# Attention: all chunks of the projected parts kept, the second part of q on GpSimd, the last head's rows moved from SBUF to SBUF, sums as rows of 64

## The chip, the cores and the metric

The kernel runs on one core of a Trainium2 chip. The metric is the device time in microseconds (us) of one execution of the whole program. Engines: TensorE (PE), VectorE (DVE), ScalarE (ACT), GpSimd (POOL) and SyncE (SP), which here only issues DMAs. SBUF and PSUM have 128 partitions.

## The reference

Eight layers act on `x`, 2048 tokens of 128 numbers: a Mamba block, a mixture of experts (MoE), causal attention, MoE, Mamba, a low-rank MLP, causal attention with ALiBi biases, and the MLP again. The change is in attention alone, which runs twice with 16 heads of 8 dimensions:

```python
q, k, v = xn @ Wq, xn @ Wk, xn @ Wv           # heads: 16 x 8 columns
dots = einsum('bhid,bhjd->bhij', q, k) * scale # second one: + alibi_bias
attn = softmax(where(causal, -inf, dots))
out  = einsum('bhij,bhjd->bhid', attn, v)
x = x + out @ Wo
```

## The kernel before

Attention cuts the 2048 tokens into four chunks of 512 (`CH`, `NC` = 4) and has three stages.

**Projection.** For each chunk `project(c)` on TensorE makes q, k and v in the PSUM tile `acc`. q and k are then written as a sum of three bf16 numbers: the first part (`first_part`) by ScalarE, what is left of it (`rest`, by `remove_first` on VectorE), the second part by ScalarE (`second`), the third part of k by VectorE (`third_of_k`) and that of q by GpSimd. The parts lie in `parts`, two chunks deep, so ScalarE waits for `stored[c - 2]` before it writes chunk c. SyncE stores each part to HBM (`store_parts`: three stores for q, one for k), waits until they have landed, and loads head 0's operands of the chunk (`load_tokens(0, ...)`) back into `q_op` and `k_op`. Then it loads heads 1 to 3.

**Heads.** For each head, a first pass of scores (`item`, tile `ps_q`) gives VectorE the row maxima (`maxes`, L1701 and L1704). TensorE starts on it after the last `project`. It visits the chunks in order, chunk c with 4(c+1) blocks. The maxima go through GpSimd, TensorE, VectorE and a DMA into `q_op`. The second pass (`scores`, tile `ps_k`) is exponentiated by ScalarE (`exps`) and multiplied by v in blocks of four (`times_v`, tile `ps_o`). ScalarE copies a finished chunk to `o_sb`; SyncE stores it to HBM (`store`). One head later `load_output` brings the head's rows back as `oT` (head dimensions on partitions) and its softmax sums as `sums`, where a partition holds one (block of 256 tokens, head) pair; one chunk uses 32 of the 128 partitions.

**Output.** The last head is loaded chunk by chunk (`load_last`). For each chunk VectorE adds the four partial sums and inverts them (`invert`), adds half of the partial rows (`add_partials`; GpSimd adds the other half into `upper`), multiplies by the spread inverses (`divide`), adds the result to `x` (`add`) and takes the norm statistics for the next layer. TensorE spreads the inverses over partitions with `sel_head` (`spread`, tile `ps_s`, L1582) and multiplies by `wo` (`output`, tile `ps_y`, L1591). `spread` and `output` of chunks 0 and 1 stand in TensorE's program between the last head's `times_v` blocks, after n = 20, 24, 28 and 32 of the 40 blocks; those of chunks 2 and 3 come after the last block.

The order on every engine is the order in which the code is written. Instructions on an engine start in that order, so a wait holds back all that is behind it.

## Time and profile before

| what | value |
|---|---|
| median of 3 runs | 2073.79 us (2072.45 to 2076.75) |
| the profiled execution | 2079.87 us, span 2077.9 us |
| TensorE busy | 1798.5 us, 87% |
| VectorE busy | 1619.0 us, 78% |
| ScalarE busy | 1117.0 us, 54% |
| GpSimd busy | 542.9 us, 26% |
| first attention | from about 520 to 1003 us of the span |
| second attention | from about 1534 to 2018 us |

The span is cut into stages with different limits, so these shares alone say little; the stages of attention have to be read one by one. In the rows below, a line has the start in us, the duration in us, the engine and line, the operation and tiles, how many were merged, and in square brackets the idle time before it and what ended that. PEld is TensorE's weight load, SPq the DMA issue on SyncE. The letters a0 and a1 in a tile's name stand for the first and the second attention.

### The profile page before, as it was taken

The page shows a single profiled execution, that of the slowest core. Times are in us where ns is not written, and L with a number is a line of the kernel's source. Part 1 is how long each engine was busy: PE and PEld are TensorE (multiplying, and loading weights), DVE is VectorE, ACT ScalarE, POOL GpSimd, SP SyncE. Part 2 cuts the span into 40 slices and gives each one's busy share as a digit, 9 for nine tenths or more (in the row PEclk, how much of TensorE's full clock was granted, in tenths as well). Part 3 has the DMA queues.
Part 4 walks back from the last instruction along what each step waited for, and adds up shares of the span by engine and source line. Part 5 has one row for each costly group of instructions (what it writes and reads, how often), then busy time and mean ns, then how long its engine had stood idle before and what let it go on. Part 6 is the DMA issues. An engine that isn't in the chain of part 4 may idle for free. (4 is left out here: it accounts for less than half of the span.)

```text
span 2077.9 us, 46457 instructions
## 1 busy us (share of the span) xinstructions
PE 1798.5 (87%) x18012; PEld 902.7 (43%) x18012; DVE 1619.0 (78%) x3425; ACT 1117.0 (54%) x2083; POOL 542.9 (26%) x560
## 2 busy tenths in 40 slices
PE   6777788999799999997899977777768999999967
PEld 2222254444255555553444422222533555555534
DVE  5899965666788999984565559999658999998665
ACT  5544423222278888885322274443342888888815
POOL 2798930000200000001000029989230000000012
PEclk9899998999689999998799979999886999999969
DMA  5333300311312222211041004443012222222200
GB/s 174 117 122 120 123 11 0 82 51 31 102 30 49 53 53 57 53 27 26 3 87 51 26 20 133 124 121 102 1 43 77 49 54 57 56 61 44 34 8 21
DMA packets 64617, 127.37 MB, mean 61 GB/s; under 512 B 15959, under 2 KB 26741, under 8 KB 62925
## 3 DMA queue, kind: packets, MB, share of 16 engines
q1 hardware_dynamic: 64108, 123.88, 23.3%
q8 instruction: 142, 2.33, 0.5%
q14 instruction: 79, 0.64, 0.1%
q10 hardware_dynamic: 288, 0.52, 0.1%
HBM read 105.74 MB, written 17.43 MB: 59 GB/s over the span
## 5 line engine op out<-in xcount | busy, mean ns | idle before, releaser
L1644 ACT ACTIVATE a_probs<-a_ps_k 128x512 f32<-128x512 f32 (+3 forms) x1280 | 598.9, 545 | 229.6 <-PE a_ps_k L1556 129.8
L1538 PE MATMUL a_ps_q<-a_k_op,a_q_op 84*32 84x512 bf16 (+7 forms) x5120 | 536.5, 366 | 29.0 <-DVE a_maxes L1701 18.8
L1704 DVE TENSOR_REDUCE a_maxes<-a_ps_q 128x1 f32<-128x512 f32 x768 | 504.1, 686 | 65.9 <-PE a_ps_q L1538 63.2
L1552 PE MATMUL a_ps_k<-a_q_op,a_k_op 87*32 87x512 bf16 (+7 forms) x5120 | 518.9, 354 | 6.2 <-DMA a_q_op<-a_max_T 2.9
L1574 PE MATMUL a_ps_o<-a_probs,a_vh 128*32 128x512 f32 (+3 forms) x2752 | 318.7, 508 | 0.8 <-ACT a_probs L1644 0.8
L1538 PEld LDWEIGHTS a_ps_q<-a_k_op,a_q_op 72*32 72x32 bf16 (+1 forms) x5120 | 187.4, 97 | 175.2 <-DVE a_maxes L1704 68.7
L1701 DVE CUSTOM_DVE_ANT_0 a_ps_q<-a_ps_q,all_c_mask_q 128x128 f32<-128x128 f32 (+3 forms) x512 | 248.0, 496 | 7.6 <-PE a_ps_q L1538 6.4
L1552 PEld LDWEIGHTS a_ps_k<-a_q_op,a_k_op 75*32 75x32 bf16 (+1 forms) x5120 | 185.7, 96 | 141.7 <-ACT a_probs L1644 84.0
L979 ACT ACTIVATE e_silu<-e_psg,all_me_b 128x512 f32<-128x512 f32 x128 | 87.8, 687 | 227.9 <-PE e_psg L911 227.9
L1784 POOL CAST a_max_parts<-a_neg_max 128x16 bf16<-128x16 f32 x32 | 6.3, 197 | 756.1 <-DVE a_neg_max L1709 756.1
L1062 DVE SCALAR_TENSOR_TENSOR e_mid<-e_psv,all_me_b,e_silu 128x512 f32<-128x512 f32 x128 | 95.7, 749 | 129.3 <-PE e_psv L913 125.4
L172 POOL TENSOR_TENSOR all_rstd<-all_var_eps,all_c_minus_half 128x4 f32<-128x4 f32 x36 | 40.1, 1114 | 503.8 <-DVE all_var_eps L161 503.8
L571 POOL TENSOR_TENSOR m0sc_read<-m0sc_state,m0sc_c_rows 128x1024 f32<-128x1024 f32 x64 | 150.3, 2360 | 11.4 <-PE m0sc_psy L490 5.8
L571 POOL TENSOR_TENSOR m1sc_read<-m1sc_state,m1sc_c_rows 128x1024 f32<-128x1024 f32 x64 | 150.2, 2358 | 9.7 <-DVE m1sc_state L536 5.5
L1556 PE MATMUL a_ps_k<-all_c_mask_k,all_c_ident_b 128*32 128x128 bf16 x2048 | 150.0, 222 | 0.9 <-issue 0.9
L536 DVE TENSOR_TENSOR_SCAN m0sc_state<-m0sc_decay,m0sc_carry,m0sc_drive 128x1024 f32<-128x1024 f32 x64 | 146.6, 2331 | 0.5 <-ACT m0sc_drive L515 0.5
L536 DVE TENSOR_TENSOR_SCAN m1sc_state<-m1sc_decay,m1sc_carry,m1sc_drive 128x1024 f32<-128x1024 f32 x64 | 146.5, 2328 | 0.4 <-ACT m1sc_drive L515 0.4
L490 PE MATMUL m0sc_psy<-m0sc_read,all_c_ident 128*128 128x512 f32 x256 | 126.1, 616 | 19.1 <-POOL m0sc_read L571 19.0
L490 PE MATMUL m1sc_psy<-m1sc_read,all_c_ident 128*128 128x512 f32 x256 | 127.5, 623 | 16.7 <-POOL m1sc_read L571 16.6
L911 PE MATMUL e_psg<-e_xT,all_me_w_T 128*128 128x512 f32 x256 | 133.9, 605 | 1.5 <-ACT e_xT L197 1.5
L913 PE MATMUL e_psv<-e_xT,all_me_w_T 128*128 128x512 f32 x256 | 132.3, 599 | 0.0
L900 PE MATMUL e_pso<-e_hid,all_me_w_T 128*128 128x512 f32 x256 | 119.2, 595 | 4.7 <-DVE e_hid L1071 4.6
(265 smaller groups left out, 2396.9 us busy)
## 6 DMA issues: line engine op xcount, KB each, us to landing
m0sc_c_rows<-m_bc_rows SPq DMA_DIRECT2D x32, 512.0 KB, 3.6
e_w_rows<-e_comb SPq DMA_DIRECT2D x64, 256.0 KB, 3.2
m1sc_c_rows<-m_bc_rows SPq DMA_DIRECT2D x32, 512.0 KB, 3.6
a_outputs<-a_o_sb SPq DMA_DIRECT2D x512, 18.0 KB
a_q_op<-a_q_parts SPq DMA_DIRECT2D x30, 288.0 KB
a_k_op<-a_k_parts SPq DMA_DIRECT2D x30, 288.0 KB
m0sc_b_rows<-m_bc_rows SPq DMA_DIRECT2D x32, 256.0 KB
m1sc_b_rows<-m_bc_rows SPq DMA_DIRECT2D x32, 256.0 KB
```

The costliest lines, as they stand in the source:

```text
L490: last = pe.matmul(psy[:, h, chunk(b)], g["ident"][:, :], read[h][:, chunk(b)], start=False, stop=q % NS == NS - 1, skip_group_check=True)
L536: dve.tensor_tensor_scan(state[half(q, h)][:, :], decay[half(q, h)][:, :], drive[:, h, :], carry[:, h, q % NS:q % NS + 1], ALU.mult, ALU.a ...
L571: pool.tensor_tensor(read[h][:, :], state[half(q, h)][:, :], c_rows[q % 2][:, :], ALU.mult).then_inc(read_ready, 1)
L911: pe.matmul(psg[:, f, :], w["w1_T"][:, e, fs], xT[:, tokens(c)], start=True, stop=True).then_inc(g_ready, 1)
L913: pe.matmul(psv[:, f, :], w["w2_T"][:, e, fs], xT[:, tokens(c)], start=True, stop=True).then_inc(v_ready, 1)
L1538: last = pe.matmul(ps_q[32 * r:32 * r + 32, use % QB, 0:width], q_op[h % SLOT][0:NR, part(t, r)], k_op[h % SLOT][0:NR, kc * CH:kc * CH + w ...
L1552: last = pe.matmul(ps_k[32 * r:32 * r + 32, b % KB, 0:width], k_op[h % SLOT][:, part(j, r)], q_op[h % SLOT][:, c * CH + first:c * CH + fir ...
L1556: last = pe.matmul(ps_k[32 * r:32 * r + 32, b % KB, 0:P], g["ident_b"][:, part(0, r)], g["mask_k"][:, :], start=False, stop=True, skip_gro ...
L1574: pe.matmul(ps_o[rows, c % 2, lo:hi], vh[h % SLOT][:, j, :], probs[:, a % PSLOT, lo - first:hi - first], start=j < 4, stop=j >= TPC * c, s ...
L1644: act.activation(probs[:, n % PSLOT, 0:width], ps_k[:, b % KB, 0:width], ACT.Exp).then_inc(exp_done, 1)
L1701: dve.tensor_tensor_reduce(bank, bank, g["mask_q"][:, CH - width:CH], 1.0, -3e38, ALU.add, ALU.max, found).then_inc(q_read, 1)
L1704: dve.tensor_reduce(found, bank, AX.X, ALU.max).then_inc(q_read, 1)
```

## The change

1. `parts` has room for all four chunks, and ScalarE no longer waits for `stored`.
2. The second part of q is made by GpSimd, directly before the third, and GpSimd's eight memsets of `vh` come after all four chunks. ScalarE keeps the second part of k.
3. VectorE makes the third part of k of chunk c-1 before `remove_first(c)`, no longer after it.
4. SyncE stores chunk c before it loads head 0's operands of chunk c-1.
5. `sums` is laid out with head and block of 64 tokens on the 128 partitions, the chunk along the row. `invert` works on 128 partitions with 64 columns. `load_output` needs four loads of sums for each head, not one; `spread` needs eight matmuls of 64 columns, not two of 256.
6. The last head's rows are no longer stored and loaded: `move_last` and `move_sums` copy them from `o_sb` to `oT` and `sums`, four DMAs each, before SyncE's `load_output(14)`. For the last chunk ScalarE issues `move_sums`.
7. `spread` and `output` of chunks 0 and 1 come one block of four later (n = 24, 28, 32, 36).

```diff
-            parts = [me.sb(n, [P, SPL, 2, CH], BF16) for n in ("q_parts", "k_parts")]
+            parts = [me.sb(n, [P, SPL, NC, CH], BF16) for n in ("q_parts", "k_parts")]
-        sums = m.sb("sums", [SB * HEADS, 4, BT])
+        sums = m.sb("sums", [HEADS * SB, NC, 4, JT])
...
+        def move_sums(eng, c):
+            for r in range(4):
+                eng.dma_start(sums[LAST * SB:(LAST + 1) * SB, c, r, :],
+                              o_sb[32 * r + DH:32 * r + DH + 1, c, :]).then_inc(last_sums[c], 16)
...
-                for b in range(BPC):
-                    last = pe.matmul(ps_s[:, b * BT:(b + 1) * BT], g["sel_head"][:, BPC * c + b, :], inv[:, :],
-                                     start=True, stop=True)
+                for j in range(SB):
+                    last = pe.matmul(ps_s[:, j * JT:(j + 1) * JT], g["sel_head"][:, j, :], inv[:, :], start=True, stop=True)
...
-                    if h == LAST and n == 20:
+                    if h == LAST and n == 24:
                         pe.wait_ge(q_read, USES)
                         spread(0)
...
-                    if c >= 2:
-                        act.wait_ge(stored[c - 2], 64)
-                    act.activation(parts[o][:, 0, c % 2, :], acc[:, o, :], ACT.Copy, scale=scale[o]).then_inc(first_part[o], 1)
+                    act.activation(parts[o][:, 0, c, :], acc[:, o, :], ACT.Copy, scale=scale[o]).then_inc(first_part[o], 1)
...
-                second(c)
+                second_of_k(c)
...
+            act.wait_ge(o_read, NC * HEADS)
+            move_sums(act, NC - 1)
...
-                rows = slice(BPC * HEADS * c, BPC * HEADS * (c + 1))
-                dve.wait_ge(last_back[c], 32)
-                dve.tensor_tensor(pair[rows, :, :], sums[rows, 0:2, :], sums[rows, 2:4, :], ALU.add).then_inc(paired, 1)
+                dve.wait_ge(last_sums[c], 16 * 4)
+                dve.tensor_tensor(pair[:, :, :], sums[:, c, 0:2, :], sums[:, c, 2:4, :], ALU.add).then_inc(paired, 1)
                 dve.wait_ge(paired, c + 1)
-                dve.tensor_tensor(inv[rows, :], pair[rows, 0, :], pair[rows, 1, :], ALU.add).then_inc(summed, 1)
+                if c:
+                    dve.wait_ge(spread_ready, c)
+                dve.tensor_tensor(inv[:, :], pair[:, 0, :], pair[:, 1, :], ALU.add).then_inc(summed, 1)
                 dve.wait_ge(summed, c + 1)
-                dve.reciprocal(inv[rows, :], inv[rows, :]).then_inc(inverted, 1)
+                dve.reciprocal(inv[:, :], inv[:, :]).then_inc(inverted, 1)
...
             def add_partials(c):
+                dve.wait_ge(last_back[c], 16 * 4)
...
             for c in range(1, NC):
+                third_of_k(c - 1)
                 remove_first(c)
-                third_of_k(c - 1)
...
-            dve.wait_ge(o_back, 16 * 2 * LAST)
+            dve.wait_ge(o_back, 16 * BACKS * LAST)
...
+            for c in range(NC):
+                pool.wait_ge(left[0], c + 1)
+                pool.tensor_copy(parts[0][:, 1, c, :], rest[0][:, c % 2, :]).then_inc(second_part[0], 1)
+                pool.wait_ge(second_part[0], c + 1)
+                pool.tensor_tensor(parts[0][:, 2, c, :], rest[0][:, c % 2, :], parts[0][:, 1, c, :],
+                                   ALU.subtract).then_inc(third_part[0], 1)
...
-                sp.dma_start(sums[h::HEADS, :, :], rows[DH, :, :].rearrange("r (b t) -> b r t", b=SB)).then_inc(o_back, 16)
+                for c in range(NC):
+                    sp.dma_start(sums[h * SB:(h + 1) * SB, c, :, :],
+                                 rows[DH, :, chunk(c)].rearrange("r (j t) -> j r t", j=SB)).then_inc(o_back, 16)
+
+            def move_last(c):
+                sp.wait_ge(o_read, NC * LAST + c + 1)
+                if c < NC - 1:
+                    move_sums(sp, c)
+                for r in range(4):
+                    sp.dma_start(oT[LAST * DH:(LAST + 1) * DH, r, chunk(c)],
+                                 o_sb[32 * r:32 * r + DH, c, :]).then_inc(last_back[c], 16)
...
+            def load_first(c):
+                sp.wait_ge(stored[c], 64)
+                load_tokens(0, chunk(c), head0_loaded[c])
             for c in range(NC):
                 store_parts(c)
-                sp.wait_ge(stored[c], 64)
-                load_tokens(0, chunk(c), head0_loaded[c])
+                if c:
+                    load_first(c - 1)
+            load_first(NC - 1)
...
-                    store(h, c)
-                    if h == LAST:
+                    if h < LAST:
+                        store(h, c)
+                    else:
+                        move_last(c)
                         if c == 0:
                             load_output(h - 1)
-                        load_last(c)
```

On SyncE, in the first attention's projection, before the change (`a_q_parts` and `a_k_parts` are the tensors in HBM, `a0pr_...` the tiles in SBUF):

```order
L1824 DMA a_q_parts<-a0pr_q_parts 16x8x512 x3
L1827 DMA a_k_parts<-a0pr_k_parts 384x1x512
L1834 DMA a_q_op_257<-a_q_parts 72x1x512
L1835 DMA a_k_op_261<-a_k_parts 72x1x512
L1824 DMA a_q_parts<-a0pr_q_parts 16x8x512 x3
L1827 DMA a_k_parts<-a0pr_k_parts 384x1x512
```

And after it:

```order
L1830 DMA a_q_parts<-a0pr_q_parts 16x8x512 x3
L1833 DMA a_k_parts<-a0pr_k_parts 384x1x512
L1830 DMA a_q_parts<-a0pr_q_parts 16x8x512 x3
L1833 DMA a_k_parts<-a0pr_k_parts 384x1x512
L1840 DMA a_q_op_258<-a_q_parts 72x1x512
L1841 DMA a_k_op_262<-a_k_parts 72x1x512
```

The two loads of a chunk now stand behind the four stores of the next one.

On SyncE, around the first attention's last head, before:

```order
L1855 DMA a_outputs<-a_o_sb 9x512 x8
L1862 DMA a_oT<-a_outputs 8x4x2048
L1863 DMA a_sums<-a_outputs 8x4x256
L1868 DMA a_oT<-a_outputs 8x4x512
L1869 DMA a_sums<-a_outputs 2x4x256
L1855 DMA a_outputs<-a_o_sb 9x512 x4
```

And after:

```order
L1861 DMA a_outputs<-a_o_sb 9x512 x4
L1496 DMA a_sums<-a_o_sb 8x1x64 x4
L1878 DMA a_oT<-a_o_sb 8x512 x4
L1868 DMA a_oT<-a_outputs 8x4x2048
L1870 DMA a_sums<-a_outputs 8x4x64 x4
L1496 DMA a_sums<-a_o_sb 8x1x64 x4
L1878 DMA a_oT<-a_o_sb 8x512 x4
```

Eight copies within SBUF stand ahead of the load of head 14, and that load has four DMAs of sums; a store and a load of the last head are gone.

On TensorE, in the first attention's last head from n = 20 on, before (`x4` of `a_ps_o` closes a block of four):

```order
L1574 MATMUL a_ps_o<-a_probs,a_vh_268 32x128
L1582 MATMUL a0ou_ps_s<-a0ou_inv,all_c_sel_head 128x256 x2
L1552 MATMUL a_ps_k<-a_q_op_260,a_k_op_264 32x512 x16
L1574 MATMUL a_ps_o<-a_probs,a_vh_268 32x512 x4
L1591 MATMUL a0ou_ps_y<-all_a_wo,a0ou_total 128x128 x4
```

And after:

```order
L1580 MATMUL a_ps_o<-a_probs,a_vh_269 32x128
L1558 MATMUL a_ps_k<-a_q_op_261,a_k_op_265 32x512 x16
L1580 MATMUL a_ps_o<-a_probs,a_vh_269 32x512 x4
L1588 MATMUL a0ou_ps_s<-a0ou_inv,all_c_sel_head 128x64 x8
L1558 MATMUL a_ps_k<-a_q_op_261,a_k_op_265 32x512 x16
L1580 MATMUL a_ps_o<-a_probs,a_vh_269 32x512 x4
L1596 MATMUL a0ou_ps_y<-all_a_wo,a0ou_total 128x128 x4
```

`spread(0)` now has one more block of attention ahead of it.

## Rows read from the trace of the kernel before

**Rows 1.** Windows: start:end, length, busy time (instructions) of each engine, PE clock, DMA

```profile
577.00:940.00 363.00, 358.71 (x6981) 211.62 (x6977) 329.60 (x846) 297.37 (x647) 14.52 (x70) 0.99 0.23 45
984.00:1004.00 20.00, 8.36 (x25) 6.00 (x26) 14.35 (x31) 0.00 (x0) 5.30 (x4) 0.56 0.03 7
```

**Rows 2.** Timeline of the first attention's projection, all engines

```profile
530.97 0.68 DVE L1686 TENSOR_TENSOR a0pr_k_parts<-a0pr_k_rest,a0pr_k_parts 128x512 bf16<-128x512 f32 x1
531.77 0.58 SPq L1827 DMA_DIRECT2D a_k_parts<-a0pr_k_parts  x1
...
534.71 0.60 ACT L1658 ACTIVATE a0pr_q_parts<-a0pr_acc 128x512 bf16<-128x512 f32 x1 [3.00 <-DMA a_k_parts<-a0pr_k_parts]
...
542.41 0.60 ACT L1658 ACTIVATE a0pr_q_parts<-a0pr_acc 128x512 bf16<-128x512 f32 x1 [4.51 <-DMA a_k_parts<-a0pr_k_parts]
...
544.24 2.24 DVE L1686 TENSOR_TENSOR a0pr_k_parts<-a0pr_k_rest,a0pr_k_parts 128x512 bf16<-128x512 f32 x2
...
544.58 1.36 POOL L1800 TENSOR_TENSOR a0pr_q_parts<-a0pr_q_rest,a0pr_q_parts 128x512 bf16<-128x512 f32 x1 [5.96 <-ACT a0pr_q_parts L1636]
...
548.91 0.84 SPq L1834 DMA_DIRECT2D a_q_op<-a_q_parts  x1
...
550.58 1.85 SPq L1824 DMA_DIRECT2D a_q_parts<-a0pr_q_parts  x3
```

**Rows 3.** Timelines of PE and DVE, head 0's first pass, first attention

```profile
553.72 1.15 PE L1538 MATMUL a_ps_q<-a_k_op,a_q_op 72*32 72x512 bf16 x12 [2.40 <-DMA a_k_op<-a_k_parts]
...
554.39 1.29 DVE L1704 TENSOR_REDUCE a_maxes<-a_ps_q 128x1 f32<-128x512 f32 x2 [2.00 <-PE a_ps_q L1538]
...
561.07 1.89 DVE L1704 TENSOR_REDUCE a_maxes<-a_ps_q 128x1 f32<-128x512 f32 x3
...
570.08 0.22 DVE L1709 TENSOR_REDUCE a_neg_max<-a_maxes 128x16 f32<-128x64 f32 x1
```

**Rows 4.** Timeline of DVE, the same place of the second attention

```profile
1566.01 1.29 DVE L1704 TENSOR_REDUCE a_maxes<-a_ps_q 128x1 f32<-128x512 f32 x2 [1.63 <-PE a_ps_q L1538]
```

**Rows 5.** Timelines of ACT, SP, DVE, POOL and PE, the last head, first attention

```profile
950.15 0.65 ACT L1650 ACTIVATE a_o_sb<-a_ps_o 128x512 f32<-128x512 f32 x1
...
952.34 0.27 SPq L1862 DMA_DIRECT2D a_oT<-a_outputs  x1
...
953.82 0.65 SPq L1869 DMA_DIRECT2D a_sums<-a_outputs  x1
...
960.32 0.68 DVE L1715 TENSOR_TENSOR a0ou_pair<-a_sums 32x512 f32<-32x512 f32 x1 [13.99 <-DMA a_sums<-a_outputs]
...
960.36 1.76 POOL L1816 TENSOR_TENSOR a0ou_upper<-a_oT 128x512 f32<-128x512 f32 x1 [18.32 <-DMA a_sums<-a_outputs]
...
964.32 2.05 PE L1582 MATMUL a0ou_ps_s<-a0ou_inv,all_c_sel_head 128*128 128x256 f32 x4 [4.74 <-DVE a0ou_inv L1719]
```

**Rows 6.** Timelines of DVE and PE, output stage of the first attention

```profile
973.66 0.41 DVE L1717 TENSOR_TENSOR a0ou_inv<-a0ou_pair 32x256 f32<-32x256 f32 x1
974.11 1.74 DVE L1719 RECIPROCAL a0ou_inv<-a0ou_inv 32x256 f32<-32x256 f32 x1
...
981.63 0.69 DVE L1738 TENSOR_TENSOR all_x<-a0ou_ps_y,all_x 128x512 f32<-128x512 f32 x1 [2.05 <-PE a0ou_ps_y L1591]
...
996.85 2.08 PE L1582 MATMUL a0ou_ps_s<-a0ou_inv,all_c_sel_head 128*128 128x256 f32 x4 [5.13 <-DVE a0ou_inv L1719]
...
1001.88 0.69 DVE L1738 TENSOR_TENSOR all_x<-a0ou_ps_y,all_x 128x512 f32<-128x512 f32 x1 [1.14 <-PE a0ou_ps_y L1591]
```

**Rows 7.** Prices: groups (count, busy us, mean ns), a timeline of MoE, the DMA queue

```profile
L1784 POOL CAST a_max_parts<-a_neg_max 128x16 bf16<-128x16 f32 x32 | 6.3, 197 | 756.1 <-DVE a_neg_max L1709 756.1
L1049 DVE RECIPROCAL e_weight<-e_weight 128x16 f32<-128x16 f32 x2 | 0.5, 253 | 0.1
...
1009.36 0.76 PEld L956 LDWEIGHTS e1ln_psl<-all_me_g_T,e_xT 128*128 128x128 f32 x3 [0.52 <-issue]
...
q1 hardware_dynamic: 64108, 123.88, 23.3%
```

More of the change, by code:

```diff
@@ L1379, in attention @@
             upper = ml.sb("upper", [P, 2, CH])
-            pair = ml.sb("pair", [P, 2, BT])
-            inv = ml.sb("inv", [P, BT])
+            pair = ml.sb("pair", [P, 2, JT])
+            inv = ml.sb("inv", [P, JT])
         q_op = [m.sb(f"q_op{s}", [NR_MAX, TOK], BF16) for s in range(SLOT)]
@@ L1391, in attention @@
         max_T = m.sb("max_T", [SPL * NT, P], BF16)
-        o_sb = m.sb("o_sb", [P, NC, CH])
         with ExitStack() as early:
@@ L1434, in attention @@
         last_back = [m.sem(f"last_back{c}") for c in range(NC)]
-        cleared = m.sem("cleared")
+        last_sums = [m.sem(f"last_sums{c}") for c in range(NC)]
         paired = m.sem("paired")
@@ L1447, in attention @@
         STORES = 4 * 16
+        BACKS = 1 + NC
         q_items = [(t, kc) for t in range(NT) for kc in range(t // TPC + 1)]
@@ L1615, in _ @@
                     times_v(h, n)
-                    if h == LAST and n == 20:
+                    if h == LAST and n == 24:
                         pe.wait_ge(q_read, USES)
                         spread(0)
-                    if h == LAST and n == 24:
+                    if h == LAST and n == 28:
                         output(0)
-                    if h == LAST and n == 28:
+                    if h == LAST and n == 32:
                         spread(1)
-                    if h == LAST and n == 32:
+                    if h == LAST and n == 36:
                         output(1)
@@ L1631, in _, with second_of_k @@
             AHEAD = 4
-            def second(c):
-                for o in range(2):
-                    act.wait_ge(left[o], c + 1)
-                    act.activation(parts[o][:, 1, c % 2, :], rest[o][:, c % 2, :], ACT.Copy).then_inc(second_part[o], 1)
+            def second_of_k(c):
+                act.wait_ge(left[1], c + 1)
+                act.activation(parts[1][:, 1, c, :], rest[1][:, c % 2, :], ACT.Copy).then_inc(second_part[1], 1)
             def exps(b):
@@ L1680, in remove_first @@
                         dve.wait_ge(third_part[o], c - 1)
-                    dve.scalar_tensor_tensor(rest[o][:, c % 2, :], acc[:, o, :], scale[o], parts[o][:, 0, c % 2, :],
+                    dve.scalar_tensor_tensor(rest[o][:, c % 2, :], acc[:, o, :], scale[o], parts[o][:, 0, c, :],
                                              ALU.mult, ALU.subtract).then_inc(left[o], 1)
@@ L1685, in third_of_k @@
                 dve.wait_ge(second_part[1], c + 1)
-                dve.tensor_tensor(parts[1][:, 2, c % 2, :], rest[1][:, c % 2, :], parts[1][:, 1, c % 2, :],
+                dve.tensor_tensor(parts[1][:, 2, c, :], rest[1][:, c % 2, :], parts[1][:, 1, c, :],
                                   ALU.subtract).then_inc(third_part[1], 1)
@@ L1797, in _ @@
                 pool.memset(vh[s][:, :, DH:DH + 1], 1.0).then_inc(v_set, 1)
-            for c in range(NC):
-                pool.wait_ge(second_part[0], c + 1)
-                pool.tensor_tensor(parts[0][:, 2, c % 2, :], rest[0][:, c % 2, :], parts[0][:, 1, c % 2, :],
-                                   ALU.subtract).then_inc(third_part[0], 1)
             pool.wait_ge(v_set, 2 * SLOT)
@@ L1823, in store_parts @@
                     sp.wait_ge(ready[0], c + 1)
-                    sp.dma_start(q_dram[:, s, :, chunk(c)], parts[0][:, s, c % 2, :]).then_inc(stored[c], 16)
+                    sp.dma_start(q_dram[:, s, :, chunk(c)], parts[0][:, s, c, :]).then_inc(stored[c], 16)
                 for ready in (first_part, second_part, third_part):
@@ L1827, in store_parts @@
                 sp.dma_start(k_dram[:, :, :, chunk(c)].rearrange("h d s t -> (h d) s t"),
-                             parts[1][:, :, c % 2, :]).then_inc(stored[c], 16)
+                             parts[1][:, :, c, :]).then_inc(stored[c], 16)
             def load_tokens(h, tokens, sem):
```

20 lines of the change are left out of this document (6 added, 14 removed).

## The prediction

> **What bounds the kernel now.** I read the busy time by stage first, then the waits, then the timeline at both ends of each attention. In the long middle of attention TensorE is busy 358.71 of 363 us [rows 1] and the change takes nothing from TensorE, VectorE or ScalarE there; what it adds is three small DMA issues a head on SyncE. So a gain can come only from the projection and the output stage, in both attentions.
>
> In the projection ScalarE stands still twice, 3.00 and 4.51 us, until a store of chunk c-2 has landed [rows 2], and all engines stop with it. The chain that matters goes on through SyncE: stores, a wait for them, the load of head 0's operands. TensorE waits 2.40 us for the load of chunk 2 and VectorE 2.00 us behind it; from there VectorE runs without a pause to head 0's last maximum at 570.08 [rows 3]. In the output stage the reader should see a chain between two engines that wait for each other: VectorE inverts, TensorE spreads, VectorE divides, TensorE multiplies, VectorE adds. It starts at 960.32, when the last head's sums are back, and TensorE has then stood still for 4.74 us at 964.32 with attention's own work behind it [rows 5].
>
> **Projection, step by step (first attention).** The buffer of four chunks takes both ScalarE waits away. Next late is the loop from one chunk's q to the next over TensorE, ScalarE and VectorE. From single instructions I estimate its period at 3.7 us (about six steps of 0.6 to 0.7 us, like those in [rows 2]). The new order on VectorE puts the third part of k (0.68 us) ahead of the next `remove_first`, so chunk 1's rest of q is ready about 531.2.
>
> GpSimd then makes q's second and third part. The third costs up to 1.36 us [rows 2]. The cast of 512 columns is not in the trace: below it lies the cast of 16 columns, 0.20 us [rows 7], above it the two-input operation of 512 columns, 1.36 us [rows 2]. I take 0.7, since it reads one input. So q's third part of chunk 1 is there at 531.2 + 0.7 + 1.4 = 533.3. The moved memsets come after it and are needed only by the second pass, some 40 us later: nothing.
>
> Now SyncE bounds. Each chunk costs it 1.85 us for three stores of q, 0.58 for k and 1.67 for the two loads (548.91 to 550.58): 4.1 us [rows 2]. From 533.3: the last store of q and that of k end at 534.5, load 0 at 536.2, stores 2 at 538.6, load 1 at 540.3, stores 3 at 542.7, load 2 at 544.4. GpSimd's third parts of chunks 2 and 3, at 3.7 us a chunk, are there at about 537 and 541, just in time. Before, load 2 was issued by 550.58 and TensorE had it at 553.72, so 3.1 us; with stores queued ahead of it on the same DMA engines I take 3.6 (bounds 3.1 and 5). TensorE to VectorE is 0.67 [rows 3]. VectorE could begin chunk 2 at 544.4 + 3.6 + 0.7 = 548.7. It must also have done chunk 1: chunk 2 takes 6.7 us and chunk 3 9.0 [rows 3], so chunk 1 about 4.4; its load lands at 540.3 + 3.6 + 0.7 = 544.6, and it ends at 549.0. Against 554.39 that is **5.4 us**. Chunk 3's load (issued by 547.5) is in time, so the whole rest moves with it. The second attention has the same picture, VectorE waiting for the same load until 1566.01 [rows 4]; I take the same 5.4. Bounds for each: 2.5 if the engines get into each other's way, 7.5 if SyncE never holds anything.
>
> Where they can: of two third parts of k that take 0.68 alone, the pair beside GpSimd's 1.36 us took 2.24, so one waited 0.9 [rows 2]. By the Trainium skill, page "SBUF — State Buffer", section "Who interferes with whom", a VectorE instruction with two SBUF inputs and a GpSimd instruction that reads SBUF exclude each other for the whole instruction. By that, a third part of k could wait for cast and subtraction, 2.1 us a chunk, and the loop would take 5.8 us, above SyncE's 4.1.
>
> **Output stage, step by step.** Start: SyncE is ready at 950.8, when chunk 0 is in `o_sb` [rows 5]. Eight copies within SBUF at 0.27 to 0.65 an issue are 2.2 to 5.2 us; I take 3.0, as the copy of rows (0.27) is the nearest to half of them. Then head 14's load: 0.27 + 4 x 0.65 = 2.9, so 956.7. A DMA issued at 531.77 had released its waiter at 534.7, 2.9 later [rows 2]; I take 2.6 after the end of the issue: VectorE starts at 959.3 in place of 960.32. Bounds 958.5 and 963. The round trip through HBM is gone, but head 14's load is behind it and lands hardly sooner.
>
> `invert`: the two additions cost 0.68 at 512 columns and 0.41 at 256, so about 0.29 at 128 and 0.21 at 64. The reciprocal costs 1.74 at 256 and 0.25 at 16 [rows 6, 7], 6.2 ns a column, so 0.55 at 64. Together with gaps 1.1 against 2.95: **1.85 us less** on VectorE for each chunk. In chunk 0 the second addition waits for GpSimd's 1.76 us all the same, so `inverted` comes 2.6 us after the start, at 961.9.
>
> `spread`: the columns are the same, 512 in all, but 8 matmuls are 16 passes with 16 weight loads, where 2 were 4. At 8 columns a pass the weight loads still come 0.21 us apart at the low clock (0.76 for three, of which the last 0.34 is its own length) [rows 7]; at the high clock I take half of that. So 16 of them, with the last one's length, are 3.6 us at 1.2 GHz and 1.9 at 2.4, against 2.08 before [rows 6], which was at the low clock (granted 0.56 of full in [rows 1]). **1.5 us more** for each chunk at the low clock.
>
> `spread(0)` comes one block later: TensorE was ready at 959.6; the block (2.3 us) brings it to 961.9, just as the inverse is there. The stall of 4.74 goes. On from there, at the high clock: spread 963.8, block 966.2, output(0) 1.1 to 967.3, VectorE's add and statistics 2.2 to 969.5, invert(1) 970.6 (TensorE has done its block by 969.7 and waits 0.9), spread(1) 972.6, last block 974.1, output(1) 975.2, add(1) 975.3. Before it was 981.63 [rows 6]: **6.3 us**, with the earlier start in it. Chunks 2 and 3 then go at the chain's pace, 10.1 us each ((1001.88 - 981.63)/2), and change by -1.85 + 1.5 = -0.35 each: **0.7 us**. Together 7.0 an attention, bounds 2 and 9 without the clock.
>
> **The sum.** 2 x (5.4 + 7.0) = 24.8 us. The profiled execution (2079.87, span 2077.9) would come to 2055.1. It lies 6.1 above the median of the runs, 2073.79; taken from the median, the forecast is **2049.0 us**.
>
> **Rivals.**
> - *The engines get in each other's way.* GpSimd and VectorE exclude each other as above and head 14's load lands at 962.5. For it: the 2.24 us pair, and four loads where one was. Then 2.5 to 3 in place of 5.4, and 3.2 less in the output stage: 2 x 5.8 less gain, 2060.6.
> - *The clock stays high to the end.* TensorE's 4.74 us idle stretch is gone. Then each of the four last chunks gets 1.7 (spread) and about 0.9 (output) more: 10.4, 2038.6. Against it: in the last chunks TensorE is busy 8.36 of 20 us [rows 1] and stays near that.
> - *Columns alone set the spread's time.* Then nothing is added: 4 x 1.5 and 4 x 0.9 less, 9.6, 2039.4. The 8-column rows speak against it. It is what the Trainium skill, page "TensorE: Matmul & The Clock Gate", section "Wait — 56ns, not 53.3ns?" gives for back-to-back matmuls, start to start the columns over the clock; its section on the back-to-back issue gap counts weight loads in too, and by that the trace agrees.
> - *The copies out of one partition go piece by piece (slower).* A row of 512 numbers becomes eight rows of 64. If a DMA moved single numbers, that were 4 x 512 pieces; the mean packet takes 0.12 us (23.3% of 16 engines' span for 64108) [rows 7], so on 8 engines some 26 us or more for each chunk. The start would move to 977, 16.7 later than before, and chunks 1 to 3 would wait about 2 us each for their own copies. All other gains are 11.4 an attention, so it decides from a start later than 971.7, and at 977 the time is 2073.8 + 2 x (16.7 + 6 - 11.4) = 2096.4. Against it: both sides have runs of 64 contiguous numbers.
> - *The projection does not get faster*, since SyncE's order costs what the buffers give: only the 14.0 of the output stage, 2059.8; counted with the first rival.
>
> **Chances.** Forecast 0.47; in each other's way 0.28; clock 0.10; columns 0.07; copies slower than before 0.04; no measurable change 0.04. Range 2036 to 2063: it leaves out the last two. About 0.2% (4 us) is what a measurement of this kernel can tell from no change. Faster 0.92, same 0.04, slower 0.04.
>
> **What would show it.** ScalarE's two waits for a store gone, VectorE's first pass of head 0 closed up, its last maximum 5 us sooner after the stage's start; GpSimd's cast near 0.7; the first pair sum at about 959 minus the projection's gain; no TensorE idle before the first spread; spread of 16 passes at 3.6 us and a reciprocal of 0.55. Wrong: a cast above 1.4, a spread of 2.1, a later start of the output stage, or a granted clock of 0.9 in the last two chunks.

## The result and the profile after

The changed kernel takes **2067.74 us** (median of 20 runs, 2062.48 to 2074.16) beside 2078.02 (20 runs, 2072.09 to 2085.93) for the kernel before on the same chip: ratio **0.9948, 95% interval 0.9935 to 0.9962**, a gain of 10.8 us (7.9 to 13.5). The forecast was a gain of 24.8 and 2049.0 us, range 2036 to 2063. The sign is right, the size is not. Of the miss in microseconds (18.7) about 4 is the base: 20 runs put the kernel before at 2078.0, three had put it at 2073.8.

The profiled executions are 16.8 us apart in span (2077.9 and 2061.1), more than the medians, so I read lengths of stages and not times since the start. The first part, the gate and the chain repeat from run to run within about 1.5 us. "First part" is from the first transpose of the stage to head 0's last maximum, "heads 0 to 15" from there to the last head's (head 15's) last maximum, "gate" from that to VectorE's first pair sum of the output stage, "chain" from the pair sum to the last add on `x`.

| us | before, att. 0 | after | before, att. 1 | after |
|---|---|---|---|---|
| first part | 49.79 | 42.74 | 48.09 | 42.10 |
| heads 0 to 15 | 370.71 | 370.18 | 374.06 | 368.61 |
| gate | 19.53 | 23.81 | 19.32 | 23.48 |
| chain | 41.56 | 39.28 | 42.50 | 38.88 |

The first part is better than forecast, the gate is worse by over 4 us, and the chain gives back half to most of that. The 5.5 us of heads 0 to 15 in the second attention are taken up below.

**Projection, first attention,** timelines of POOL, DVE, PE and SP (start, length, engine, line, what; in brackets idle time and what ended it):

```profile
533.37 0.61 POOL L1799 CAST a0pr_q_parts<-a0pr_q_rest 128x512 bf16<-128x512 f32 x1 [1.21 <-DVE a0pr_q_rest L1685]
534.06 1.16 POOL L1801 TENSOR_TENSOR a0pr_q_parts<-a0pr_q_rest,a0pr_q_parts 128x512 bf16<-128x512 f32 x1
...
532.62 0.68 DVE L1685 SCALAR_TENSOR_TENSOR a0pr_q_rest<-a0pr_acc,a0pr_q_parts 128x512 f32<-128x512 f32 x1
...
534.60 1.17 DVE L1690 TENSOR_TENSOR a0pr_k_parts<-a0pr_k_rest,a0pr_k_parts 128x512 bf16<-128x512 f32 x1 [0.70 <-ACT a0pr_k_parts L1640]
535.69 0.68 DVE L1685 SCALAR_TENSOR_TENSOR a0pr_q_rest<-a0pr_acc,a0pr_q_parts 128x512 f32<-128x512 f32 x1
...
543.36 0.75 SPq L1841 DMA_DIRECT2D a_k_op<-a_k_parts  x1
...
547.09 1.15 PE L1544 MATMUL a_ps_q<-a_k_op,a_q_op 72*32 72x512 bf16 x12 [0.76 <-DMA a_k_op<-a_k_parts]
...
563.20 0.22 DVE L1713 TENSOR_REDUCE a_neg_max<-a_maxes 128x16 f32<-128x64 f32 x1
```

The loop goes round in 3.07 us (532.62 to 535.69; forecast 3.7) and the cast takes 0.61 (0.7). Load 2 is issued by 544.11 (544.4), TensorE waits 0.76 for it where it had waited 2.40 [rows 3]. VectorE's third part of k takes 1.17 beside GpSimd's 1.16, and 0.68 alone: it ends 0.55 after GpSimd, nearly as if it had begun when GpSimd was done. By the Trainium skill, page "SBUF — State Buffer", section "Who interferes with whom", the port pair that GpSimd shares with VectorE is an exclusive lock; the trace agrees with it for this pair of instructions. The cast is no test of it: the third part of k needs ScalarE's second part, which was ready at 534.56, after the cast had ended (533.98). The 0.5 us a chunk did not bound the projection.

**The last head, first attention,** timelines of SP, DVE and PE:

```profile
943.41 2.75 SPq L1496 DMA_DIRECT2D a_sums<-a_o_sb  x4
946.21 2.67 SPq L1878 DMA_DIRECT2D a_oT<-a_o_sb  x4
949.03 0.35 SPq L1868 DMA_DIRECT2D a_oT<-a_outputs  x1
949.43 1.33 SPq L1870 DMA_DIRECT2D a_sums<-a_outputs  x4
...
957.19 0.29 DVE L1718 TENSOR_TENSOR a0ou_pair<-a_sums 128x128 f32<-128x128 f32 x1 [21.48 <-DMA a_sums<-a_outputs]
957.51 1.17 DVE L1722 TENSOR_TENSOR a0ou_inv<-a0ou_pair 128x64 f32<-128x64 f32 x1
958.71 0.55 DVE L1724 RECIPROCAL a0ou_inv<-a0ou_inv 128x64 f32<-128x64 f32 x1
...
959.41 3.64 PE L1588 MATMUL a0ou_ps_s<-a0ou_inv,all_c_sel_head 128*128 128x64 f32 x16 [5.07 <-DVE a0ou_inv L1724]
```

Two windows of the same place (start:end, length, busy time of PE, PEld, DVE, ACT and POOL, granted clock, DMA share, GB/s):

```profile
954.50:959.40 4.90, 0.00 (x0) 0.02 (x1) 2.14 (x4) 0.49 (x1) 1.36 (x1) 0.66 0.15 18
959.40:963.20 3.80, 3.79 (x20) 3.60 (x24) 1.14 (x3) 0.00 (x0) 0.00 (x0) 0.50 0.10 18
```

The eight copies take 5.47 us on SyncE (943.41 to 948.88), 0.67 to 0.69 each; I had taken 3.0. Head 14's load is issued in 1.73, 1.9 with the gap before it (2.9 taken), and VectorE starts 6.43 us after the end of that issue (2.6 taken). So TensorE, ready at 954.34, stands for 5.07 us as it did before (4.74, [rows 5]). Its granted clock falls to 0.50 of full, which is 1.2 GHz, and the first spread takes 3.64.

**A later chunk,** timelines of DVE and PE:

```profile
981.73 0.69 DVE L1734 TENSOR_TENSOR a0ou_total<-a0ou_total,a0ou_upper 128x512 f32<-128x512 f32 x1 [1.22 <-POOL a0ou_upper L1822]
983.80 0.69 DVE L1739 TENSOR_TENSOR a0ou_total<-a0ou_total,a0ou_ps_s 128x512 f32<-128x512 f32 x1 [1.38 <-PE a0ou_ps_s L1588]
...
986.66 0.69 DVE L1744 TENSOR_TENSOR all_x<-a0ou_ps_y,all_x 128x512 f32<-128x512 f32 x1 [1.14 <-PE a0ou_ps_y L1596]
...
989.83 3.67 PE L1588 MATMUL a0ou_ps_s<-a0ou_inv,all_c_sel_head 128*128 128x64 f32 x16 [3.21 <-DVE a0ou_inv L1724]
...
996.47 0.69 DVE L1744 TENSOR_TENSOR all_x<-a0ou_ps_y,all_x 128x512 f32<-128x512 f32 x1 [1.15 <-PE a0ou_ps_y L1596]
```

The period, from one add on `x` to the next, is 9.81 (986.66 to 996.47) in place of 10.1 [rows 6], as worked out.

### The profile page after: what moved, and what is told of

Read it like the earlier page. It is cut to its first block and busy times, and to the rows that moved or that the text cites. A ratio compares the mean times of both kernels' runs of the same rounds, so it can differ in the third digit from the quotient of the medians.

```text
span 2061.1 us, 46755 instructions
## 1 busy us (share of the span) xinstructions
PE 1801.9 (87%) x18108; PEld 914.8 (44%) x18108; DVE 1600.7 (78%) x3423; ACT 1112.6 (54%) x2075; POOL 545.0 (26%) x568
## 5 line engine op out<-in xcount | busy, mean ns | idle before, releaser
L490 PE MATMUL m0sc_psy<-m0sc_read,all_c_ident 128*128 128x512 f32 x256 | 126.1, 616 | 18.7 <-POOL m0sc_read L571 18.6
```

The lines of the kernel that those rows point to most:

```text
L490: last = pe.matmul(psy[:, h, chunk(b)], g["ident"][:, :], read[h][:, chunk(b)], start=False, stop=q % NS == NS - 1, skip_group_check=True)
```

## Experiments: which half gains, which loses

The projection's half alone, put into the kernel before:

```diff
-            parts = [me.sb(n, [P, SPL, 2, CH], BF16) for n in ("q_parts", "k_parts")]
+            parts = [me.sb(n, [P, SPL, NC, CH], BF16) for n in ("q_parts", "k_parts")]
...
+                pool.tensor_copy(parts[0][:, 1, c, :], rest[0][:, c % 2, :]).then_inc(second_part[0], 1)
...
+                third_of_k(c - 1)
                 remove_first(c)
-                third_of_k(c - 1)
...
+                if c:
+                    load_first(c - 1)
+            load_first(NC - 1)
```

> The kernel before with the projection's half of the change alone (parts of all chunks, GpSimd's second part of q, loads of head 0 one chunk later). In the trace of the changed kernel head 0's last maximum of the first attention stands 7.0 us sooner after the stage's start than before. Theory L (the whole loss lies in the output stage, whose start is late): this kernel gains the 7 us in both attentions and keeps them, since its output stage is that of before: 13 to 14 us, about 2064.5 by the median of 2078.0. Rival S (part of the projection's gain is given back later in the attention, or in the next stage): head 0 is 7 us sooner as well, but the kernel gains 10 us or less, 2068 or more.

Measured: ratio 0.9900 (0.9876 to 0.9924), 21 us less (16 to 26), more than the whole change gives and more than theory L's 13 to 14. First part 42.40 and 41.65 (first and second attention, here and below); gate 20.06 and 19.58. About 3 us more are found below, in the second attention's first heads; that makes 16 to 17, at the lower end of the interval.

The output stage's half alone, all of the change but the above; its core:

```diff
-                for b in range(BPC):
...
+                for j in range(SB):
...
-                    if h == LAST and n == 20:
+                    if h == LAST and n == 24:
...
-                    store(h, c)
-                    if h == LAST:
+                    if h < LAST:
+                        store(h, c)
+                    else:
+                        move_last(c)
...
-                        load_last(c)
```

> The kernel before with the output stage's half alone (sums as rows of 64, last head's rows copied within SBUF, spread one block later). Theory L: VectorE's first pair sum comes 4.2 us later after the last head's last maximum (23.7 in place of 19.5 us), the chain from there to the end is 2.3 us shorter, so each attention is about 2 us longer, 4 in all: 2082, slower by 0.2%. Rival S: the output stage is no loss by itself, 2078 or less, down to 2064 if its steps were as forecast (7.0 an attention).

Measured: ratio 1.0023 (1.0007 to 1.0039), 4.8 us **slower** (1.5 to 8.1); first part 49.77 and 47.66, gate 24.00 and 23.68, chain 38.87 and 39.39. Theory L holds for both in direction: the projection is the gain, the output stage a loss. The two add up to -16, the whole change gives -10.8; the intervals leave room for that difference.

## Experiments: what the start of the output stage waits for

The last head through HBM as before, the sums in the new layout:

```diff
-                        move_last(c)
+                        store(h, c)
                         if c == 0:
                             load_output(h - 1)
+                        load_last(c)
```

> The changed kernel with the last head's rows sent through HBM as before (four stores and two loads a chunk in place of eight copies), in the new layout of the sums. Theory L: the start is as in the kernel before, 19.5 us after the last head's last maximum in place of 23.8, and everything behind it stays: 4.3 us an attention, 8.6 in all, about 2059. Rival: the start is set by head 14's load with its four DMAs of sums, which this kernel keeps; then it gains less than 2 us an attention, 2064 or more.

Measured: ratio 0.9901 (0.9876 to 0.9926), 2062.19; gate 21.97 and 21.26, 1.8 and 2.2 sooner than with the copies but not 19.5. By its time this kernel is some 10 us ahead of the changed one (4 to 16), as theory L said; by its stages it is 5.7 ahead (gate 4.1, chain 1.7), and the gate, which theory L is about, does not come back to that of before. The copies cost part of the delay, and what is left goes with head 14's load and its four DMAs of sums. So the place of that load had to be looked at, and not the route of the last rows alone.

Head 14's load ahead of the copies:

```diff
-                        move_last(c)
                         if c == 0:
                             load_output(h - 1)
+                        move_last(c)
```

> The changed kernel with head 14's load (one DMA of rows, four of sums) issued ahead of the last head's first eight copies. In the changed kernel the eight copies took 5.4 us on SyncE, the load's issue ended at 950.8, and VectorE started at 957.2, 6.4 later. Theory A (what lands late is head 14's load of 256 KB): it is out 5.4 us sooner, the last copy of chunk 0 ends its issue about 951.7 at the latest and lands within 2.6, so VectorE starts about 954.5, 2.7 us sooner an attention, 5.4 in all: about 2062. Theory B (any of these transfers takes some 6 us to be seen, the copies too): the start moves to 957 to 958, the time does not change, 2067.7.

Measured: ratio 0.9872 (0.9849 to 0.9895), 2057.60. The gate is 21.22 and 20.52, 2.6 and 3.0 sooner, as theory A has it. The chain is shorter as well, 36.31 and 36.62, which I had not expected: TensorE stands for 1.54 us only and the first spread then takes 1.97. Gate and chain explain 10.8 us against the changed kernel; the two ratios are 16 us apart, with an interval of about 10 to 21 that still holds the 10.8.

Head 14 chunk by chunk, with a semaphore for each chunk:

```diff
+                dve.wait_ge(h14_back[c], 32)
...
-            dve.wait_ge(o_back, 16 * BACKS * LAST)
+            dve.wait_ge(o_back, 16 * BACKS * (LAST - 1))
...
+                        if c == 0:
+                            for e in range(NC - 1):
+                                load_14(e)
                         move_last(c)
                         if c == 0:
-                            load_output(h - 1)
+                            load_14(NC - 1)
```

> The changed kernel with head 14 loaded chunk by chunk, each with its own semaphore: chunks 0 to 2 ahead of the last head's first copies (their stores landed long before), chunk 3 behind those copies. Nothing of head 14 then stands between the last head's chunk 0 and the start. The four copies of sums end their issue 2.8 us after SyncE starts them. Theory A (a copy is seen 4.1 us after its issue, as in the run with head 14 first; head 14's load was the longer wait): VectorE starts about 17 us after the last maximum in place of 23.8, the inverse is there before TensorE has ended its block, so TensorE's stall of 5.07 us is gone and the first spread runs at the high clock; the attention is 6 to 7 us shorter, 13 in all, 2054 to 2055. Theory B (the landing of the copies themselves takes some 10 us and bounds the start): start at 21 or later, gain 3 an attention.

Measured: ratio 0.9865 (0.9852 to 0.9878), 2053.61. Timelines of SP, DVE and PE, first attention:

```profile
947.68 2.75 SPq L1497 DMA_DIRECT2D a_sums<-a_o_sb  x4
950.47 2.67 SPq L1889 DMA_DIRECT2D a_oT<-a_o_sb  x4
...
951.72 0.29 DVE L1720 TENSOR_TENSOR a0ou_pair<-a_sums 128x128 f32<-128x128 f32 x1 [14.19 <-DMA a_sums<-a_o_sb]
...
954.51 0.69 DVE L1733 TENSOR_TENSOR a0ou_total<-a_oT 128x512 f32<-128x512 f32 x1 [1.65 <-DMA a_oT<-a_o_sb]
...
956.09 2.00 PE L1589 MATMUL a0ou_ps_s<-a0ou_inv,all_c_sel_head 128*128 128x64 f32 x16
```

The gate is 16.53 and 16.38. A copy within SBUF releases its waiter 1.3 to 1.4 us after the end of its issue here (950.43 to 951.72, 953.14 to 954.51), sooner than theory A's 4.1; in the last experiment below it is 1.8 and 2.3 for the copies of sums. So in the kernels with one load of head 14, that load was the late one: VectorE starts 5.6 to 7.1 us after the end of its issue in the eight kernels that have both that load and the copies. It is 256 KB of rows and four DMAs of sums, 8 KB each; no run tells the two apart. By the Trainium skill, page "DMA: Bandwidth & Descriptors", section "Anatomy of one DMA — SWDGE (gpsimd) path", most of a transfer's fixed 2 us is the receipt from the memory written to, HBM's being the heaviest. The order agrees here, for the queue of SyncE: 1.3 to 1.4 us into SBUF, and 3.7 from the issue of head 14's last store into HBM (943.12) to what waited for it (946.83) in the run with that load first, 2.9 in its second attention. TensorE has no wait ahead of the first spread, and runs it at the high clock (2.00 us in place of 3.64).

Spreads and outputs back at their old places:

```diff
-                    if h == LAST and n == 24:
+                    if h == LAST and n == 20:
                         pe.wait_ge(q_read, USES)
                         spread(0)
+                    if h == LAST and n == 24:
+                        output(0)
                     if h == LAST and n == 28:
-                        output(0)
+                        spread(1)
                     if h == LAST and n == 32:
-                        spread(1)
-                    if h == LAST and n == 36:
                         output(1)
```

> The changed kernel with the two spreads and outputs back at their old places in TensorE's order, one block sooner (after items 20, 24, 28, 32). The prediction held that the later place takes away the stall ahead of the first spread. If it were so, this costs about 4 us an attention. Theory L (VectorE starts at 23.8 whatever TensorE does, so the place only says how long TensorE stands): the stall is one block longer, 7.4 us in place of 5.1, the block is done later in another gap, and the time changes by less than 1 us an attention.

Measured: ratio 0.9945 (0.9930 to 0.9960), as the changed kernel; the stall is 7.58 us (5.07), the chain 38.13 and 38.14, a little shorter than the 39.28 and 38.88 of the later places, the gate 24.14 and 24.80, a little longer. The place only says how long TensorE stands.

## Experiments: what a spread costs, and the clock

Rows of 128, with `sel_head` and the tiles of the sums to match:

```diff
-        JT = CH // SB
+        SR = 4
+        JT = CH // SR
...
-                for j in range(SB):
+                for j in range(SR):
```

> The changed kernel with rows of 128 in place of 64: 64 partitions, 4 matmuls of 128 columns (8 passes) in place of 8 of 64 (16 passes), a reciprocal of 128 columns. If each pass costs a weight load of 0.21 us at the low clock, the spread is about 2.1 us in place of 3.66, the reciprocal 0.95 in place of 0.55; with VectorE's wait for GpSimd's upper sum that is 1.2 us less for each chunk at the low clock (three of four), 3.5 us an attention, 7 in all: about 2061. Rival (the spread is bound by its columns, the 3.66 have another cause): the spread stays near 3.6 and the kernel is 0.5 us slower a chunk, 4 in all: 2072.

Measured: ratio 0.9911 (0.9893 to 0.9930), 2061.61. Timelines of POOL, DVE and PE:

```profile
977.46 1.38 POOL L1823 TENSOR_TENSOR a0ou_upper<-a_oT 128x512 f32<-128x512 f32 x1
...
976.95 0.94 DVE L1725 RECIPROCAL a0ou_inv<-a0ou_inv 64x128 f32<-64x128 f32 x1
977.82 1.57 DVE L1732 TENSOR_TENSOR a0ou_total<-a_oT 128x512 f32<-128x512 f32 x1
...
986.75 2.07 PE L1589 MATMUL a0ou_ps_s<-a0ou_inv,all_c_sel_head 64*128 64x128 f32 x8 [3.78 <-DVE a0ou_inv L1725]
```

The spread takes 2.07 at the low clock and 1.16 at the high one; the period falls from 9.81 to 8.80, 1.0 in place of the 1.2 expected, since VectorE's lower sum now meets GpSimd's upper sum and takes 1.57 in place of 0.63. The rival falls. A matmul on fp32 data is two passes through TensorE here. At the low clock a pass of 64 columns cost 0.23 us (3.67 / 16), one of 128 costs 0.26 (2.07 / 8), and one of 256 cost 0.52 (2.08 / 4, [rows 6]). Halving the columns from 256 to 128 halves a pass; halving them again takes off only 0.03.

Idle work on TensorE in its gaps:

```diff
+            def fill(c, n):
+                if c >= 2:
+                    pe.wait_ge(added, c - 1)
+                for i in range(n):
+                    pe.matmul(ps_y[:, c % 2, :], q_op[LAST % SLOT][0:NR, 0:P], k_op[LAST % SLOT][0:NR, 0:CH], start=True,
+                              stop=True, skip_group_check=True)
...
+                        fill(0, 20)
                         spread(0)
...
+                        fill(1, 3)
                         spread(1)
...
             for c in range(2, NC):
+                fill(c, 12)
                 spread(c)
+                fill(c, 3)
                 output(c)
```

> The changed kernel with idle work on TensorE in its gaps (20 matmuls of 512 bf16 columns ahead of the first spread, 3 ahead of the second, 12 ahead of the third and fourth, 3 ahead of the last two outputs; their results are not read). It prices the clock in the output stage. Where the clock stays at its high level the spread takes 2.0 in place of 3.65, the output 1.1 in place of 2.08: 1.7 us in chunk 0, 2.3 in chunks 2 and 3 (VectorE then waits for GpSimd's upper sum), 6 us an attention, 12 in all: 2055 to 2056. Rival (the granted clock falls all the same): 12 matmuls then take 5.1 us in a gap of 3.2, and each of the last two chunks is 2 us longer, 8 in all: 2076.

Measured: ratio 0.9887 (0.9866 to 0.9907), 2056.62, 13 us less than the changed kernel by the ratios (12 expected). Window of the last chunks (columns as above), then the timeline of PE:

```profile
977.00:993.00 16.00, 12.99 (x80) 8.19 (x78) 12.54 (x41) 0.00 (x0) 5.25 (x4) 1.00 0.03 5
```

```profile
987.95 2.00 PE L1595 MATMUL a0ou_ps_s<-a0ou_inv,all_c_sel_head 128*128 128x64 f32 x16 [0.62 <-DVE a0ou_inv L1735]
...
991.13 1.16 PE L1603 MATMUL a0ou_ps_y<-all_a_wo,a0ou_total 128*128 128x128 f32 x8 [0.53 <-DVE a0ou_total L1750]
```

In the first attention's last chunks the granted clock is 1.00, the spread takes 2.00, the output 1.16, and the period is 7.55 in place of 9.81: 2.26 us a chunk, as worked out (2.3). The 20 matmuls ahead of the first spread did not reach all the way in the first attention: TensorE still waited 1.29 us and that spread took 3.09; in the second it took 2.00. The prediction's clock rival had its price right (1.7 and 0.9), and nothing in this change brings it about: in the changed kernel the third and fourth spread take 3.67.

## Experiments: inside the projection

SyncE's old order in the changed kernel:

```diff
                 store_parts(c)
-                if c:
-                    load_first(c - 1)
-            load_first(NC - 1)
+                load_first(c)
```

> The changed kernel with SyncE's order of before: a chunk's stores, a wait until they have landed, then its load of head 0's operands. Theory O (SyncE's order gives part of the gain): SyncE's step a chunk is about 6.5 us in place of 4.1, load 2 is issued about 2.7 us later (by 546.8 in place of 544.1 in the first attention), and the first head's last maximum comes 2 to 2.7 us later in each attention, 4 to 5 in all. Rival (the buffers alone gave the 7 us): no change.

Timeline of PE, first attention:

```profile
548.63 1.15 PE L1544 MATMUL a_ps_q<-a_k_op,a_q_op 72*32 72x512 bf16 x12 [3.20 <-DMA a_k_op<-a_k_parts]
```

Measured: ratio 0.9993 (0.9973 to 1.0012): without the new order of the loads the change as a whole gains nothing that can be seen. First part 46.90 and 45.67 in place of 42.74 and 42.10, so the order is worth 4.2 and 3.6. The rest of the new projection is worth about 2.3 (from 49.3 and 47.9, the means of the three kernels with the old projection, down to these). TensorE waits 3.20 us for load 2 (0.76 with the new order), as the timeline shows. My 2 to 2.7 was too low.

Second part of q back on ScalarE:

```diff
+                for o in range(2):
+                    act.wait_ge(left[o], c + 1)
+                    act.activation(parts[o][:, 1, c, :], rest[o][:, c % 2, :], ACT.Copy).then_inc(second_part[o], 1)
...
-                pool.tensor_copy(parts[0][:, 1, c, :], rest[0][:, c % 2, :]).then_inc(second_part[0], 1)
```

> The changed kernel with q's second part back on ScalarE (the buffers of four chunks and the order of the loads kept). In the changed kernel the loop from one chunk to the next takes 3.1 us, GpSimd's cast 0.61 of it beside the loop. Theory P (moving the cast off ScalarE matters, since ScalarE is in the loop with five operations of about 0.65 a chunk): the first head's last maximum comes 1 to 2 us later in both attentions, 2 to 4 us in all. Rival Q (the engines get in each other's way: VectorE's third part of k takes 1.16 beside GpSimd, 0.68 alone, so with less on GpSimd VectorE is faster): no later or up to 1 us sooner.

Measured: ratio 0.9938 (0.9916 to 0.9960); first part 41.99 and 42.94, 0.8 sooner and 0.8 later than the changed kernel. Theory P falls: GpSimd's second part gives nothing that can be seen. Load 2 ends its issue 23.3 us after the start of the stage here and 23.7 in the changed kernel, so the load leaves at the same time with either engine: SyncE issues without a pause ahead of it (538.23 to 544.11 in the changed kernel).

Heads 0 to 15 of the second attention are 5.5 us shorter than before, and a part of that repeats from kernel to kernel: the stretch from head 0's to head 1's last maximum is 29.8 and 29.7 us with the old projection and 26.2 to 27.7 with the whole new one (29.0 with the new one and the loads in the old order). The prediction has nothing of it. In the kernel before, TensorE waited there for head 0's maxima (timeline of PE, second attention):

```profile
1591.44 0.62 PE L1552 MATMUL a_ps_k<-a_q_op,a_k_op 87*32 87x512 bf16 x4 [2.88 <-DMA a_q_op<-a_max_T]
```

So I moved their DMA, in the kernel before:

```diff
-            for h in range(1, SLOT):
+            for h in range(1, SLOT - 1):
                 load(h)
             load_maxima(0)
+            load(SLOT - 1)
```

> The kernel before, with head 0's maxima written to q_op ahead of the load of head 3 on SyncE, in place of behind it. In the second attention of the kernel before TensorE waited 2.88 us for these maxima (their DMA was issued at 1584.68, TensorE had them at 1591.44), behind the loads of three heads; in the changed kernel, whose loads are 17 us sooner, there is no such wait, and the stretch from head 0's to head 1's last maximum is 26.2 us in place of 29.8. Theory W (the maxima queue behind the loads on the DMA engines): here that stretch is 27 us or less. Rival (it is the low granted clock or something else in that stretch): it stays at 29 to 30.

Measured, one execution (2080.29 us, inside the scatter of the kernel before): the stretch is 26.7 us in place of 29.8, and TensorE's wait is gone, as theory W has it. The loads of heads 1 to 3 end their issue at 1577.4 in the kernel before and at 1560.4 in the changed one; the maxima are sent 7.3 and 11.6 us later. Windows from there on, first the kernel before, then the changed one (columns as above; the last two are the DMA share and GB/s):

```profile
1584.70:1591.44 6.74, 3.71 (x32) 0.80 (x29) 4.72 (x13) 0.00 (x0) 0.00 (x0) 0.50 0.16 62
```

```profile
1571.98:1578.00 6.02, 5.87 (x76) 2.10 (x76) 5.09 (x15) 1.43 (x4) 0.00 (x0) 0.50 0.02 5
```

Before, the DMA engines still move 62 GB/s behind the maxima's issue, far more than the 12 KB of maxima, so the loads were not through; in the changed kernel they were. So the projection's half gains a further 3 us in the second attention.

## Experiment: both remedies together

Head 14 by chunks, the idle work (3 ahead of the second spread, 12 and 3 for the last two chunks), and on GpSimd:

```diff
             for c in range(NC):
...
                 pool.tensor_tensor(upper[:, c % 2, :], oT[:, 2, chunk(c)], oT[:, 3, chunk(c)], ALU.add).then_inc(upper_ready, 1)
-                ahead.power(pool, c)
+                if c:
+                    ahead.power(pool, c - 1)
+            ahead.power(pool, NC - 1)
```

> The changed kernel with three edits of the output stage together: head 14 loaded by chunks (as in the run of that name), idle work on TensorE ahead of the last two spreads and outputs and three matmuls ahead of the second spread, and GpSimd's upper sum of the next chunk ahead of its power of this one. By the stages of the two single runs: start 16.5 us after the last maximum in place of 23.8, the first add 9.8 behind it, then periods of 7.6 to 7.8 in place of 9.8 for the last two chunks, or 7.3 where VectorE no longer waits 1.22 for the upper sum. Theory: both gains add up, 6.9 + 4.6 = 11.5 us an attention against the changed kernel, 23 in all, 2067.7 - 23 = 2045 (0.5 less a chunk with the upper sum, 2042). Rival (the filler or the earlier upper sum disturbs VectorE or TensorE): only one of the two gains is left, 2054.

Measured: 2039.04, ratio **0.9802** (0.9780 to 0.9824), 41 us less than the kernel before and 30 less than the changed kernel by the ratios (25 to 36), where 23 to 26 were expected. Gate 16.53 and 16.10, chain 32.02 and 32.43, period 7.22: VectorE no longer waits for the upper sum. Both gains add up: gate and chain together are 14.5 and 13.8 us shorter than in the changed kernel, 28 us in all.

## Why the prediction was wrong

*Projection: right mechanism, too small.* 5.4 an attention was forecast; over the nine kernels with the whole new projection and the three with the old one the first part averages 42.6 against 49.3 and 42.0 against 47.9, so 6.7 and 5.9. Loop and landing were faster (3.1 for 3.7, and 3.0 for 3.6 from the end of load 2's issue to TensorE). Most of it is SyncE's new order (4.2 and 3.6); GpSimd's second part of q, which the prediction also worked through, is worth nothing that can be seen. The maxima behind the loads gave 3 more in the second attention. Together about 16 in place of 10.8.

*Start of the output stage: the step that failed.* From the end of chunk 0's copy into `o_sb` the prediction summed 3.0 (eight copies issued) + 2.9 (head 14's load issued) + 2.6 (landing), 8.5 in all. Measured were 5.5 + 1.9 + 6.4, 13.8 in all. So VectorE started 4 us later than before, where the prediction had 1 us sooner. The landing was read from a DMA of the projection, though [rows 5] had the same kind of load in the same place: the last issue ended at 954.47 and VectorE started at 960.32, 5.9 later. Head 14's own load had ended its issue at 953.27 (timeline of SP, kernel before), 7.0 earlier than that start:

```profile
952.66 0.61 SPq L1863 DMA_DIRECT2D a_sums<-a_outputs  x1
```

The copies were priced by the row nearest to half of them, at the cheap end; two of the three terms were at the wrong end of what the trace offered. Loading head 14 ahead of the copies, and then by chunks, took 2.6 to 3.0 and 7.1 to 7.3 us off the gate, which shows that this load was what the start waited for. The start was bounded at 963 from above; with the actual terms it would have been 964.6, outside.

*The stall that goes.* It rested on the start. TensorE reached the spread as forecast (21.0 us after the last maximum), the inverse came 5 us late, and the run with the old places shows that the move itself is worth nothing. TensorE stood for 5.07 us in place of 4.74. With the stall the high clock went too: 3.64 for the first spread in place of 1.9, and a slower block behind it.

*Inverse, spread, period: right.* Reciprocal 0.55, pair 0.29, spread 3.67 and 2.00 (3.6 and 1.9 forecast), period -0.3. GpSimd's upper sum as a new wait of VectorE (1.22) was not seen; it lies beside the spread at the low clock and costs nothing there. With TensorE kept busy it is what VectorE waits for, and moving GpSimd's power behind it took the period from 7.55 to 7.23.

*Sum.* Gate and chain together are 1.6 us an attention longer (mean of four kernels with the changed output stage against three with the old one), forecast -7.0. So -16 + 3 = -13, beside a measured -10.8 (-7.9 to -13.5). The first rival named two causes. One of them, head 14's load landing late, was the true one; it was put at 962.5 (964.6 by the terms measured) and priced at 3.2 us with nothing lost behind it. The other, a projection of 2.5 to 3 us, was wrong by more than twice. That its gain of 13.2 us lies near the measured one is luck: its projection was too small and its output stage too good.

*A slip in a rival.* The copies going piece by piece were priced at 26 us a chunk; 4 x 512 pieces of 0.12 us on 8 engines are 31. The copies showed nothing of the kind, so it changes nothing here.

## What to carry to other kernels

Price a transfer's landing by a row of the same size from the same place of the program, and the issue of many small DMAs by the dearer row until one of that kind is seen. Before moving an engine's work to close a stall, ask what it waits for; remove that load from the wait (split it by chunk, send what is ready early), and the stall and the low clock behind it go together.

## What the hardware showed unexpectedly

A copy of sums from SBUF to SBUF costs SyncE 0.67 to 0.69 us an issue, a load of sums from HBM 0.33 (1.33 / 4), but the copy releases its waiter 1.3 to 2.3 us after the issue, where head 14's load (256 KB and its sums) takes 5.6 to 7.1. An fp32 pass of 64 columns is hardly cheaper than one of 128: 0.23 and 0.26 us at 1.2 GHz, 0.125 (2.00 / 16) and 0.145 (1.16 / 8) at 2.4. VectorE's sum of 512 columns takes 0.63 us alone and 1.57 when it begins 0.36 after GpSimd's 1.38 us sum; the wait shows as a longer instruction, not as idle time. A head in the middle takes 24.4 us, but in each profiled execution one to six of them take 0.6 to 3.6 more. In eight of the fourteen kernels the stretch from head 3's to head 4's last maximum in the first attention is one of them or nearly (24.9 to 25.4); the others lie mostly at other places each time. This may be part of why single executions differ by some us. In the kernel before, one such place is a wait of TensorE for nothing that the profile shows:

```profile
927.94 0.29 PE L1552 MATMUL a_ps_k<-a_q_op,a_k_op 75*32 75x256 bf16 x2 [0.95 <-issue]
```
